# Attention by head pairs in plain single precision and row tiles, in a kernel of convolutions, attention and experts

## The chip, the cores and the metric

The kernel runs on one core of a Trainium2 chip. The time is that of the device in microseconds, from one execution of the program; lower is better. Engines are named as the profile names them: PE is TensorE, DVE is VectorE, ACT is ScalarE, POOL is GpSimd, SP is SyncE; PSUM is the memory that PE writes, in 8 banks of 512 single-precision columns.

## What is computed

The input is a batch of 8 images of 64 channels and 16 x 16 points (`B, C, HH, WW = 8, 64, 16, 16`). In order:

- group norm and a deformable 3 x 3 convolution (offsets and masks from a convolution of their own, four-corner interpolation), added to the input;
- group norm, a 3 x 3 convolution and a small mixing matrix that is balanced by 20 rounds of dividing its rows and columns by their sums (40 half steps); the result is a sum of the convolution, its input and the residual, weighted by the gates and by the trace of the balanced matrix;
- layer norm and causal attention with 8 heads over the 256 points of each image, added to the tokens;
- layer norm and a mixture of 8 experts (two are chosen a token, GELU), a windowed attention sum, layer norm, a mixture of 16 gated experts (SiLU), each added.

Attention, which the change is about, comes down to this for each image and head, where Y is the normed tokens (256 x 64) and A and M are products of weights (64 x 64) that the kernel makes itself once:

```python
q      = Y @ A[head]                      # query and key weights in one matrix
scores = (q @ Y.T) * 64 ** -0.5           # causal mask
probs  = softmax(scores)
out   += probs @ (Y @ M[head])            # value and output weights in one matrix
```

## The kernel before, in words

Every engine has its own list of instructions, written by hand in `hybrid_kernel`, and semaphores between them; nothing is reordered by a scheduler. What the lists have in common is a table of *fills*: pieces of work outside the step loop (projections, transposes, gate products) that `attention_fills(s)` assigns to a step, and that each engine's loop calls up at that step. All fills in `FILLS` share PSUM bank 7: a fill may be written when the one before it has been copied out (`take`, L1974: a wait for `misc_free`). Query and value projections with an odd index are *side* fills in bank 2, with semaphores of their own.

The stages that matter here:

**Tap loop** (PE L1893, 36 steps of 9 taps for 4 image pairs). DVE makes interpolation weights, PE transposes them into PSUM, ACT copies them (L908), PE multiplies (`interpolate`, L1861). DVE adds the result to each image pair (`x1_image`, L1217), and begins to balance the first mixing matrix (`half_steps(0, ...)`, L1282) in pieces whose borders are `HALVES`.

**Between tap loop and attention.** PE runs the first 3 x 3 convolution (`conv(0, ...)`, L1926: 9 taps, two passes each, bank 1), the products of the attention weights (`attention_weights`, L1939), which it runs twice so that ACT can split the result in a high part `AVH` and a low part `AVL`, and the second convolution (`conv(1, ...)`, bank 2). DVE balances to the end (L1359, L1361), adds the convolution (`add_conv`, L1363) and the residual (`second_residual`, L1376), takes the transposed tokens (`take_tokens`, L1381), norms them (`ln_center`, `ln_variance`, `ln_out`) and copies the transposed norm `yA` to `YTs` (`ln_evac`, L1440). Ten half steps of the second matrix are done on DVE as well; the other 30 belong to POOL and DVE together in the first 17 steps of attention: POOL adds up the sums, DVE takes the reciprocal (`inverse`, L1302), POOL multiplies (L637 to L655).

**Attention**, 64 steps s, one head of one image each (image a = s // 8, head g = s % 8). The order on PE (L2096) in step s: transposes of the probabilities of head s-1 (L2103, 3 tiles), scores of head s+1 (`scores`, L2082), probabilities times values of head s-2 (L2118 to L2120), then the fills of step s. Scores go to bank s % 2, transposes to banks 3 and 4, values to banks 5 and 6. DVE (L1568) masks and scales the scores and takes the row maximum (L1573, L1577: `masked_ready`), then does the fills of step s-1, norms, and the gates of tokens. ACT (L958) takes two exponentials with row sums (L968), copies the transposed probabilities of head s-1 to one of three buffers `PTs` (L953), then the projections of step s.

The norms, queries and attention weights are in a high and a low part that together fill the 128 rows (64 channels each): tokens `YTs` hold both, and a score tile is two accumulating matmuls with `QH` and `QL`. ACT copies a query projection to `QH` (L945), and DVE subtracts that from PSUM for `QL` (`query_remainders`, L1460, L1468). `normalise` (L1472) divides by the row sums, four heads at a time; POOL adds the heads up (`fold`, L711) and splits the expert weights (`split_stage`, L738).

**Experts** (PE L2197 on), behind the last mask. `gate_wide`, the buffer of spread gates that SP fills by DMA, lies over `QH`.

## Time and profile before

| | us |
|---|---|
| median of 3 runs | 490.46 |
| lowest and highest | 490.11, 490.84 |
| the profiled execution | 486.73 |
| its span, first to last instruction | 484.9 |

| chain of work that ended last | share of the span |
|---|---|
| PE | 63% |
| DVE | 16% |
| ACT | 8% |
| issue | 6% |
| POOL, DMA | 4%, 2% |

The granted PE clock is 0.98 of full speed on average, DMA moves 43 GB/s on average. The chain is followed back from the last instruction, at each step to what released it. Busy time is the time in which an engine has an instruction in work; matmuls are pipelined, and one that is recorded with 0.4 us may be followed by the next after 0.1. In a timeline row, the first number is the start in us from the span's start, the second how long the row lasts, then engine, line, operation, the tiles out<-in, sizes, and the count of instructions that were merged in the row; in brackets the idle time before it and who ended it. In a row by stage, each engine's busy time is followed by its number of instructions.

### The profile page before, as it was taken

To read this page: it belongs to the slowest core of one execution; us is meant where nothing else is said; L and a number is where in the kernel's file an instruction comes from. 1 tells how busy PE (TensorE), PEld (TensorE's weight loads), DVE (VectorE), ACT (ScalarE), POOL (GpSimd) and SP (SyncE) were. 2 spreads that over 40 slices of the span, in tenths; PEclk is the share of its full clock that TensorE was granted. 3 is DMA by queue.
4 is the path that set the end of the run, shared out by engine and by line. 5 is a ranking of instruction groups with operands and counts; after the bars stand their busy time and mean duration, and the time that the engine had idled before them with its cause. 6 is when DMAs were issued, how large, how long until landed. Compare 5 with 4: busy or idle time off the path is not lost.

```text
span 484.9 us, 9115 instructions
## 1 busy us (share of the span) xinstructions
PE 434.6 (90%) x2998; PEld 303.3 (63%) x2998; DVE 347.4 (72%) x1090; ACT 283.1 (58%) x676; POOL 175.6 (36%) x305
## 2 busy tenths in 40 slices
PE   2999999999968988979999988999989888998994
PEld 1787777767467887979898944344435444545542
DVE  4178998867777656788978853637666888797862
ACT  3467776732557876758788855765655333343431
POOL 4400001203134563383793342415341454343342
PEclk9998999999989998989999999999999999999998
DMA  7300000000400000012300004212112213041330
GB/s 178 144 2 1 2 0 1 1 2 0 87 3 1 1 2 1 2 39 51 69 20 3 1 3 141 63 39 68 43 38 74 68 45 105 28 122 66 99 102 11
DMA packets 13567, 20.94 MB, mean 43 GB/s; under 512 B 4592, under 2 KB 6384, under 8 KB 13008
## 3 DMA queue, kind: packets, MB, share of 16 engines
q1 hardware_dynamic: 13056, 19.99, 14.4%
q10 hardware_dynamic: 464, 0.37, 0.3%
q8 instruction: 24, 0.39, 0.3%
q14 instruction: 23, 0.19, 0.1%
HBM read 19.62 MB, written 0.72 MB: 42 GB/s over the span
## 4 chain that ended last, share of the span: by engine, by line
PE 63%; DVE 16%; ACT 8%; issue 6%; POOL 4%; DMA 2%; POOLq 0%; DVEq 0%; SPq 0%; ACTq 0%
PE PS L2171 14%; PE PS L1871 7%; PE PS L1909 6%; PE PS L2182 5%; PE PS L2193 5%; PE PS L1930 3%; PE PS L2103 3%; PE PS L2091 2%; PE PS L1829 2%; PE PS L1998 2%; PE PS L2013 2%; PE PS L2047 2%; ACT score_arena L968 2%; DVE QL L1468 2%; DVE score_arena L1577 2%
## 5 line engine op out<-in xcount | busy, mean ns | idle before, releaser
L2171 PE MATMUL PS<-YTs,WH 64*128 64x512 f32 x192 | 77.0, 427 | 1.9 <-ACT VV L1067 1.6
L735 POOL TENSOR_TENSOR pr<-pr 128x512 f32<-128x512 f32 x39 | 50.4, 1291 | 75.9 <-DVE pr L1630 44.7
L2171 PE MATMUL PS<-YX,WH 64*128 64x512 f32 x192 | 77.2, 426 | 0.0
L968 ACT ACTIVATE score_arena<-score_arena,nmx 128x128 f32<-128x128 f32 (+1 forms) x128 | 56.9, 446 | 22.2 <-DVE nmx L1577 21.8
L1067 ACT ACTIVATE VV<-PS 128x512 f32<-128x512 f32 x64 | 35.4, 595 | 41.6 <-PE PS L2171 41.5
L1023 ACT ACTIVATE stage<-PS,wk 128x512 f32<-128x512 f32 x64 | 40.8, 684 | 22.8 <-PE PS L2171 22.7
L1743 DVE TENSOR_TENSOR stage<-VV,PS 128x512 f32<-128x512 f32 x64 | 41.8, 682 | 17.1 <-ACT VV L1067 12.5
L2171 PEld LDWEIGHTS PS<-YTs,WH 64*128 64x128 f32 x192 | 35.3, 184 | 29.6 <-ACT VV L1067 12.6
L908 ACT ACTIVATE st_mem<-PS 128x512 f32<-128x512 f32 x72 | 37.3, 612 | 18.5 <-PE PS L1909 18.5
L2103 PE MATMUL PS<-cst,score_arena 128*128 128x128 f32 x192 | 34.4, 290 | 6.6 <-ACT score_arena L968 6.1
L2091 PE MATMUL PS<-YTs,QH 128*128 128x128 f32 (+1 forms) x128 | 38.9, 328 | 0.0
L2171 PEld LDWEIGHTS PS<-YX,WH 64*128 64x128 f32 x192 | 35.3, 184 | 4.0
L2171 PE MATMUL PS<-YX,WL 64*128 64x512 f32 x96 | 37.5, 391 | 0.0
L2171 PE MATMUL PS<-YTs,WL 64*128 64x512 f32 x96 | 37.5, 391 | 0.0
L2193 PE MATMUL PS<-stage,wk 128*64 128x512 f32 x128 | 34.5, 617 | 2.7 <-DVE stage L1743 2.7
L2091 PE MATMUL PS<-YTs,QL 128*128 128x128 f32 (+1 forms) x128 | 36.4, 285 | 0.0
L2182 PE MATMUL PS<-stage,wk 128*64 128x512 f32 x128 | 34.5, 617 | 1.6 <-ACT stage L1023 1.2
L1871 PE MATMUL PS<-st_mem,U 128*64 128x256 f32 x288 | 33.5, 383 | 0.0
L1323 DVE TENSOR_TENSOR prod<-hats 128x768 f32<-128x768 f32 x36 | 32.0, 949 | 0.1
L716 POOL TENSOR_TENSOR pr<-pr 128x512 f32<-128x512 f32 (+2 forms) x24 | 20.1, 837 | 32.9 <-DVE pr L1481 31.4
L953 ACT ACTIVATE score_arena<-PS 128x384 f32<-128x384 f32 x64 | 30.1, 471 | 0.9 <-PE PS L2103 0.9
L1468 DVE TENSOR_TENSOR QL<-PS,QH 128x512 fp32r<-128x512 f32 x32 | 22.0, 686 | 12.1 <-ACT QH L945 12.0
(277 smaller groups left out, 1130.1 us busy)
## 6 DMA issues: line engine op xcount, KB each, us to landing
QH<-gate_store SPq DMA_DIRECT2D x96, 128.0 KB, 2.9
stage<-in_wexp SPq DMA_DIRECT2D x6, 512.0 KB, 5.9
wk<-in_w SPq DMA_DIRECT2D x1, 1034.0 KB, 9.8
wa<-in_wat SPq DMA_DIRECT2D x1, 768.0 KB, 8.1
out<-X SPq DMA_DIRECT2D x16, 32.0 KB, 1.9
cst<-in_consts SPq DMA_DIRECT2D x1, 483.0 KB, 6.4
wc<-in_w SPq DMA_DIRECT2D x2, 183.5 KB, 5.8
score_arena<-in_wcv SPq DMA_DIRECT2D x2, 144.0 KB, 6.2
```

What stands on the lines that cost most here:

```text
L735: nc.gpsimd.tensor_tensor(acc[:, c % 2], acc[:, c % 2], weighted[:, u % 2], ALU.add).then_inc(acc_added, 1)
L908: nc.scalar.activation(ST[:, i % ST_TAPS, h].rearrange("p t s -> p (t s)"), PS[:, T_BANKS[m % 6], :], ACT.Copy).then_inc(st_copied, 1)
L968: ins = nc.scalar.activation(PR[:, s % 3, cols], MS[:, s % 3, cols], ACT.Exp, bias=nmx[:, s % 3, qt:qt + 1], scale=-1.0, accum_out=rsum[:, ...
L1023: nc.scalar.activation(hid[:, n % 4], PS[:, HID_BANKS[n % 4], :], ACT.Gelu, bias=wk[:, W128["b1"]][:, r:r + 1]).then_inc(gelu_done, 1)
L1067: nc.scalar.activation(sil[:, n % 4], PS[:, SILU_BANKS[n % 2], :], ACT.Silu).then_inc(silu_done, 1)
L1743: nc.vector.tensor_tensor(hid[:, n % 4], sil[:, n % 4], PS[:, V_BANKS[n % 3], :], ALU.mult).then_inc(prod3_done, 1)
L1871: ins = mm(PS[h * C:(h + 1) * C, 5 + j % 2, 0:S], U[:, 4 * j + 2 * qt + h, k * C:(k + 1) * C], ST[:, v % ST_TAPS, h, qt], start=(k + qt == ...
L2091: ins = mm(PS[:, s % 2, cols], w[:, a % 2, g, qt * P:(qt + 1) * P], YTs[:, a * S:a * S + (qt + 1) * P], start=(r == 0), stop=(r == 1))
L2103: ins = nc.tensor.transpose(PS[:, 3 + v % 2, k * P:(k + 1) * P], PR[:, v % 3, k * P:(k + 1) * P], ident)
L2171: ins = mm(PS[:, banks[i], :], w[hs, m, tiles[i] * P:(tiles[i] + 1) * P], ys[i][hs, cs], start=(k == 0), stop=(k == 2))
L2182: ins = mm(PS[i * C:(i + 1) * C, OUT_BANKS[u % 2], :], wk[:, W128["w2_2"]][:, r * C:(r + 1) * C], hid[:, (2 * q + i) % 4], start=(ht == 0) ...
L2193: ins = mm(PS[i * C:(i + 1) * C, OUT_BANKS[u % 2], :], wk[:, W128["w3"]][:, e * C:(e + 1) * C], hid[:, (2 * r + i) % 4], start=True, stop= ...
```

## The change

- Attention goes in 32 pairs of heads. Scores of a pair are plain single precision in two row tiles: head 2m in rows 0 to 63 and bank 0, head 2m+1 in rows 64 to 127 and bank 1. `Q`, `AV` and the tokens `YA` are single precision, `YA` with the same 64 channels in both halves. `QH`, `QL`, `AVH`, `AVL`, the second run of the attention weights and the query remainders are gone.
- An image has three projections (two of queries, one of values) instead of six, each two row-tiled matmuls in banks 6 and 7. There is no side bank: every fill takes the one slot.
- ACT takes all copies of fills in attention (projections, transposed norms and tokens, the second images' gates `gS` and trace `cB`), behind the exponentials of the next pair; DVE keeps the gate products `gB`, four steps late (`LAG`).
- Order on PE in pair m: scores of pair m+1, transposes of pair m, values of pair m-1, fills. On ACT: copies of pair m-1, exponentials of pair m, fills of pair m-1. On DVE: two masks, then all other work of the two steps (`background`).
- `PTs` has four buffers; transposes go to banks 2 and 3, values to banks 4 and 5.
- The first convolution runs inside the tap loop (after taps 33, 34, 35, bank 5). The second is split by the first projections; ACT copies half of its result aside (`HC`).
- All 40 half steps of the second matrix are POOL's with DVE's reciprocals, two a step over 20 steps; the gates of the second images come at s = 2.
- The first norms of attention are one DVE product (`ln_both`) instead of three operations. `gate_wide` has a buffer of its own.

Lines that are only "..." stand for what is left out.

```diff
-    return [("q", a, i) for i in range(HPAIRS)] + [("v", a, i) for i in range(PT)]
-
-
-def on_side(name):
-
-    return name[2] % 2 == 1
-
-
-DIAG_AT, XT_AT, YA_AT = 18, (20, 27), (7, 25, 38)
-DVE_HALVES = 10
-POOL_HALVES = tuple(min(40, DVE_HALVES + 2 * s - (s > 3) - (s > 4)) for s in range(19))
-MID_INVERSE, END_INVERSE = [s for s in range(17) if s != 4], [s for s in range(15) if s != 3]
+    return [("q", a, 0), ("q", a, 1), ("v", a, 0)]
+
+
+DIAG_AT, XT_AT, YA_AT = 20, (23, 30), (6, 27, 38)
+DVE_HALVES = 0
+GATES_AT = 6
+GATE_INVERSE_AT = 3
+LAG = 4
+LN_AT = ((2, 26, 34), (3, 27, 35), (5, 28, 37))
+ADD_AT, RESIDUAL_AT = 12, 24
+POOL_HALVES = tuple(min(40, 2 * s) for s in range(21))
+MID_INVERSE, END_INVERSE = range(20), range(20)
...
-    return {0: (2, 3, 4, 5, 6, 7), 3: (2, 3, 4, 5, 6, 7)}.get(a, (0, 1, 2, 3, 4, 5))
+    return {0: (2, 4, 6), 3: (5, 6, 7)}.get(a, (1, 3, 5))
...
+    if s == GATES_AT:
+        out.append(("gS", 0))
     if s == DIAG_AT:
         out.append(("cB", 0))
-    if s < 2:
-        out.append(("q", 0, 2 + s))
+    if s == 0:
+        out.append(("q", 0, 1))
+    if a + 1 < IMAGES and i in projections_at(a):
+        out.append(projections(a + 1)[projections_at(a).index(i)])
...
-HALVES = (8, 20, 25, 30, 36)
+HALVES = (6, 34, 38)
 PE_GROUP, PE_SQUARE, PE_COEF = 23, 26, 29
+CONV_AT = (33, 34, 35)
+CONV_SPLIT = (4, 5, 6)
...
-                        pool.wait_ge(balanced, 2)
+                    if n == 0:
+                        pool.wait_ge(exp_ready, 2)
...
+                if s == 2:
+                    batch_gates(1)
...
+            project(FIRST_PROJECTIONS[0])
+            batch_exp(1)
+            project(FIRST_PROJECTIONS[1])
+            copy_tokens(1)
...
+            for m in range(STEPS // 2 + 1):
+                if m >= 1:
+                    copy_probs(2 * m - 2)
+                    copy_probs(2 * m - 1)
+                if m == 1:
+                    act.wait_ge(conv_ready, 2)
+                    nc.scalar.activation(HC[:].rearrange("p j s -> p (j s)"), PS[:, 5, :], ACT.Copy).then_inc(conv_saved, 1)
+                if m < STEPS // 2:
+                    exponentials(2 * m)
+                    exponentials(2 * m + 1)
+                for s in (2 * m - 2, 2 * m - 1) if m >= 1 else ():
                     for name in attention_fills(s):
                         if name[0] in ("q", "v"):
                             project(name)
...
-            half_steps(0, HALVES[2], HALVES[3])
-            copy_square(1)
-            half_steps(0, HALVES[3], HALVES[4])
-            copy_logits(1)
-            half_steps(0, HALVES[4], 2 * SINKHORN)
+            half_steps(0, HALVES[2], 2 * SINKHORN)
...
+            def ln_both(c):
+
+                ts = ln_ready(c)
+                nc.vector.tensor_tensor(Y2[:, ts, 0:2 * C].rearrange("p t (r c) -> p t r c", r=2), Y[:, ts].unsqueeze(2).to_broadcast([P, CHUNK, 2, C]),
+                                        lnst[:, 2, ts].unsqueeze(2).unsqueeze(3).to_broadcast([P, CHUNK, 2, C]), ALU.mult).then_inc(y2_ready, 1)
...
             second_residual(0)
-            half_steps(1, 0, 2)
-            gate_inverse(1)
             take_tokens(0)
             ln_center(0)
             ln_variance(0)
-            ln_out(0, False)
+            copy_square(1)
+            ln_both(0)
             second_residual(1)
-            half_steps(1, 2, 4)
             ln_evac("yA", 0)
-            add_conv(2)
-            add_conv(3)
-
-            queries = [0]
-
-            def query_remainders(name):
-                _, a, i = name
-                queries[0] += 1
-                if on_side(name):
-                    dve.wait_ge(side_filled, SIDE[name] + 1)
-                else:
-                    dve.wait_ge(misc_filled, FILL[name] + 1)
-                dve.wait_ge(qh_copied, queries[0])
-                nc.vector.tensor_tensor(QL[:, a % 2, 2 * i:2 * i + 2, :].rearrange("p g n -> p (g n)"), PS[:, 2 if on_side(name) else 7, :],
-                                        QH[:, a % 2, 2 * i:2 * i + 2, :].rearrange("p g n -> p (g n)").bitcast(F32),
-                                        ALU.subtract).then_inc(side_free if on_side(name) else misc_free, 1)
+            copy_logits(1)
...
+            def background(s):
+
+                a, g = divmod(s, HEADS)
+                if s == GATE_INVERSE_AT:
+                    gate_inverse(1)
                 if s in MID_INVERSE:
                     inverse()
-                nc.vector.tensor_tensor_reduce(MS[:, s % 3, P:3 * P], PS[:, s % 2, P:3 * P], c_("causal"), -SCALE, 1e30,
-                                               ALU.add, ALU.min, nmx[:, s % 3, 1:2]).then_inc(masked_ready, 1)
-                if s >= 1:
-                    take_fills(s - 1)
-                if s == DIAG_AT + 1:
+                if s >= LAG:
+                    take_fills(s - LAG)
+                if s == ADD_AT:
+                    add_conv(2)
+                    add_conv(3)
+                if s == RESIDUAL_AT:
+                    dve.wait_ge(misc_free, FILL["cB", 0] + 1)
                     second_residual(2)
                     second_residual(3)
...
+            for m in range(STEPS // 2):
+                mask_scores(2 * m)
+                mask_scores(2 * m + 1)
+                background(2 * m)
+                background(2 * m + 1)
...
+                if i in CONV_AT:
+                    if i == CONV_AT[0]:
+                        pe.wait_ge(conv_block_loaded, 32)
+                        pe.wait_ge(x1_tile_ready, 3)
+                    n = CONV_AT.index(i)
+                    conv(0, n * TAPS // len(CONV_AT), (n + 1) * TAPS // len(CONV_AT))
...
             def project(name):
                 kind, a, i = name
-                if not on_side(name):
-                    take(*name)
-                elif SIDE[name]:
-                    pe.wait_ge(side_free, SIDE[name])
-                else:
-                    pe.wait_ge(conv_added, J)
-                bank = 2 if on_side(name) else 7
-                if kind == "q":
-                    for g in (2 * i, 2 * i + 1):
-                        for r, w in enumerate((AVH, AVL)):
-                            ins = mm(PS[:, bank, (g % 2) * S:(g % 2 + 1) * S], w[:, g * P:(g + 1) * P], YTs[:, a * S:(a + 1) * S],
-                                     start=(r == 0), stop=(r == 1))
-                else:
-                    for r, w in enumerate((AVH, AVL)):
-                        ins = mm(PS[:, bank, :], YTs[:, (2 * a + i) * P:(2 * a + i + 1) * P], w[:, 2 * 512:3 * 512], start=(r == 0), stop=(r == 1))
-                ins.then_inc(side_filled if on_side(name) else misc_filled, 1)
+                take(*name)
+                for r in range(2):
+                    rs = slice(r * C, (r + 1) * C)
+                    if kind == "q":
+                        g = 4 * i + 2 * r
+                        ins = mm(PS[:, 6 + r, 0:S], AV[rs, g * C:(g + 2) * C], YA[rs, a * S:(a + 1) * S], start=True, stop=True)
+                    else:
+                        ins = mm(PS[:, 6 + r, :], YA[rs, (2 * a + r) * P:(2 * a + r + 1) * P], AV[rs, 512:1024], start=True, stop=True)
+                ins.then_inc(misc_filled, 1)
...
             def scores(s):
                 a, g = divmod(s, HEADS)
-                if g % 2 == 0:
-                    wait_projection(("q", a, g // 2))
+                if g % 4 == 0:
+                    pe.wait_ge(misc_free, FILL["q", a, g // 4] + 1)
                 if s >= 2:
-                    pe.wait_ge(masked_ready, s - 1)
+                    pe.wait_ge(masked_ready, s)
                 for qt in range(PT):
                     cols = slice(0, P) if qt == 0 else slice(P, 3 * P)
-                    for r, w in enumerate((QH, QL)):
-                        ins = mm(PS[:, s % 2, cols], w[:, a % 2, g, qt * P:(qt + 1) * P], YTs[:, a * S:a * S + (qt + 1) * P],
-                                 start=(r == 0), stop=(r == 1))
-                ins.then_inc(scores_ready, 1)
-
+                    for h in range(2):
+                        hs = slice(h * C, (h + 1) * C)
+                        ins = mm(PS[:, h, cols], Q[hs, a % 2, g // 2, qt * P:(qt + 1) * P], YA[hs, a * S:a * S + (qt + 1) * P], start=True, stop=True)
+                        if qt == 1:
+                            ins.then_inc(scores_ready, 1)
+
+            transpose_x(0)
+            square_means(1)
+            conv(1, 0, CONV_SPLIT[0])
+            coefficients(1)
+            transpose_y("yA", 0)
+            conv(1, CONV_SPLIT[0], CONV_SPLIT[1])
+            pe.wait_ge(av_copied, 1)
+            pe.wait_ge(misc_free, FILL["yA", 0] + 1)
+            project(FIRST_PROJECTIONS[0])
+            conv(1, CONV_SPLIT[1], CONV_SPLIT[2])
             scores(0)
-            for s in range(STEPS + 2):
-                if 1 <= s <= STEPS:
-                    v = s - 1
-                    pe.wait_ge(probs_ready, v + 1)
-                    if v >= 2:
-                        pe.wait_ge(pT_copied, v - 1)
-                    for k in range(3):
-                        ins = nc.tensor.transpose(PS[:, 3 + v % 2, k * P:(k + 1) * P], PR[:, v % 3, k * P:(k + 1) * P], ident)
-                    ins.then_inc(pT_ready, 1)
-                if s + 1 < STEPS:
-                    scores(s + 1)
-                if s >= 2:
-                    v = s - 2
-                    a, g = divmod(v, HEADS)
-                    if g % 4 == 0 and a >= 1:
-                        pe.wait_ge(heads_normed, 2 * a - 1 + g // 4)
-                    if g == 0:
-                        wait_projection(("v", a, 0))
-                        wait_projection(("v", a, 1))
-                    pe.wait_ge(pT_copied, v + 1)
-                    vh = slice(g * C, (g + 1) * C)
-                    o = PS[:, 5 + g // 4, (g % 4) * P:(g % 4 + 1) * P]
-                    mm(o[:, 0:C], PTs[:, v % 3, 0:P], VV[:, a % 2, 0, vh], start=True, stop=True)
-                    mm(o[:, C:P], PTs[:, v % 3, P:2 * P], VV[:, a % 2, 0, vh], start=True, stop=False)
-                    mm(o[:, C:P], PTs[:, v % 3, 2 * P:3 * P], VV[:, a % 2, 1, vh], start=False, stop=True).then_inc(pv_done, 1)
-                if s < STEPS:
-                    for what in attention_fills(s):
-                        if what[0] in ("q", "v"):
-                            project(what)
-                        elif what[0] in ("yA", "yB", "zB"):
-                            transpose_y(*what)
-                        elif what[0] == "xT":
-                            transpose_x(what[1])
-                        elif what[0] == "cB":
-                            pe.wait_ge(v3_diag_ready, 2)
-                            take(*what)
-                            mm(PS[:, 7, 0:2], spread, V3[0:B, 1, BATCHES[1], 0], start=True, stop=True).then_inc(misc_filled, 1)
-                        else:
-                            pe.wait_ge(swl_ready, 3)
-                            small_projection(*what, "wg2", E2)
+            project(FIRST_PROJECTIONS[1])
+            conv(1, CONV_SPLIT[2], TAPS)
+            transpose_x(1)
...
+            for m in range(STEPS // 2 + 1):
+                if m + 1 < STEPS // 2:
+                    scores(2 * m + 2)
+                if m < STEPS // 2:
+                    transpose_probs(2 * m)
+                    transpose_probs(2 * m + 1)
+                if m >= 1:
+                    values(2 * m - 2)
+                    values(2 * m - 1)
+                if m < STEPS // 2:
+                    for s in (2 * m, 2 * m + 1):
+                        for what in attention_fills(s):
+                            fill_attention(what)
```

## Rows read from the trace of the kernel before

**Rows 1.** The page: busy us, share of the span and instructions of each engine.

```profile
PE 434.6 (90%) x2998; PEld 303.3 (63%) x2998; DVE 347.4 (72%) x1090; ACT 283.1 (58%) x676; POOL 175.6 (36%) x305
```

**Rows 2.** Busy time by stage: length, each engine, then clock and DMA.

```profile
138.20:184.90 46.70, 41.66 (x323) 38.67 (x323) 30.79 (x143) 35.91 (x117) 23.74 (x100) 0.96 0.01 2
184.90:262.70 77.80, 70.77 (x560) 66.73 (x560) 62.66 (x247) 58.90 (x197) 47.70 (x75) 0.96 0.13 29
262.70:276.50 13.80, 13.35 (x118) 12.78 (x118) 12.20 (x60) 12.07 (x46) 5.14 (x6) 1.00 0.01 2
```

**Rows 3.** PE timeline, one step without fills (start us, us, what).

```profile
265.17 0.50 PE L2103 MATMUL PS<-cst,score_arena 128*128 128x128 f32 x3
265.42 0.30 PE L2091 MATMUL PS<-YTs,QH 128*128 128x128 f32 x1
...
265.97 0.33 PE L2118 MATMUL PS<-VV,score_arena 128*128 128x64 f32 x2
...
266.58 0.50 PE L2103 MATMUL PS<-cst,score_arena 128*128 128x128 f32 x3
```

**Rows 4.** DVE timeline ahead of attention: balancing done, tokens, residual, first mask.

```profile
120.23 0.22 DVE L1361 TENSOR_SCALAR V<-cst,V 8x4 f32<-8x4 f32 x1
...
123.45 0.36 DVE L1384 COPY T<-PS 128x256 f32<-128x256 f32 x1
...
127.45 0.48 DVE L1378 SCALAR_TENSOR_TENSOR X<-score_arena,CB,X 128x256 f32<-128x256 f32 x1
...
138.15 0.29 DVE L1573 CUSTOM_DVE_ANT_0 score_arena<-PS,cst 128x128 f32<-128x128 f32 x1
```

**Rows 5.** ACT timeline: the first exponential.

```profile
139.05 0.40 ACT L968 ACTIVATE score_arena<-score_arena,nmx 128x128 f32<-128x128 f32 x1 [3.38 <-DVE nmx L1577]
```

**Rows 6.** Chain that ended last: first convolution passes, first expert products.

```profile
106.41 3.63 PE PS L1930 x8
...
279.82 0.91 PE PS L2171 x6
```

**Rows 7.** PE timeline of the weights' product: lower and upper row group.

```profile
111.30 0.27 PE L1944 MATMUL PS<-wa 64*128 64x128 f32 x1
111.35 0.27 PE L1949 MATMUL PS<-wa 64*128 64x64 f32 x1
111.41 0.27 PE L1944 MATMUL PS<-wa 64*128 64x128 f32 x1
```

**Rows 8.** PE timeline of the expert stage: row-tiled pairs after another shape.

```profile
304.11 0.50 PE L2171 MATMUL PS<-YTs,WH 64*128 64x512 f32 x1
...
304.44 0.39 PE L2171 MATMUL PS<-YTs,WL 64*128 64x512 f32 x1
...
304.68 0.39 PE L2171 MATMUL PS<-YX,WH 64*128 64x512 f32 x1
```

**Rows 9.** DVE timeline in attention: a mask's start, the remainder behind it.

```profile
147.87 0.29 DVE L1573 CUSTOM_DVE_ANT_0 score_arena<-PS,cst 128x128 f32<-128x128 f32 x1
...
148.43 0.69 DVE L1468 TENSOR_TENSOR QL<-PS,QH 128x512 fp32r<-128x512 f32 x1
```

**Rows 10.** ACT timeline in attention: exponentials, probabilities, query copy.

```profile
148.55 0.40 ACT L968 ACTIVATE score_arena<-score_arena,nmx 128x128 f32<-128x128 f32 x1 [0.34 <-DVE nmx L1577]
...
149.44 0.47 ACT L953 ACTIVATE score_arena<-PS 128x384 f32<-128x384 f32 x1
149.81 0.58 ACT L945 ACTIVATE QH<-PS 128x512 fp32r<-128x512 f32 x1
```

**Rows 11.** DVE timeline: multiplications of two half steps that follow each other.

```profile
134.55 0.16 DVE L1293 TENSOR_TENSOR ef<-ef,mn 8x16 f32<-8x16 f32 x1
...
135.15 0.18 DVE L1293 TENSOR_TENSOR ef<-ef,mn 8x16 f32<-8x16 f32 x1
```

**Rows 12.** POOL timeline: multiplications of two half steps, with DVE.

```profile
149.82 0.21 POOL L654 TENSOR_TENSOR ef<-ef,mn 8x16 f32<-8x16 f32 x1 [0.28 <-DVE mn L1306]
...
150.84 0.21 POOL L654 TENSOR_TENSOR ef<-ef,mn 8x16 f32<-8x16 f32 x1 [0.28 <-DVE mn L1306]
```

339 lines of the change are left out of this document (167 added, 172 removed).

## The prediction, made before the changed kernel was run

> Notation: PE is TensorE, DVE VectorE, ACT ScalarE, POOL GpSimd, SP SyncE. A step is one head of one image (64 of them, s = 0 to 63), a pair is two steps (m = 0 to 31). A fill is a projection, transposition or gate product that PE slips between the steps.
>
> **What bounds the kernel now.** First the page's busy times: PE works 434.6 us of a span of 484.9, 90% [rows 1], so the question is where its time goes and where it still waits. Then busy time by stage, with the borders at the first mask of step 0, that of step 20, and the exponentials of steps 54 and 63 [rows 2]: in steps 0 to 19 PE works 41.7 of 46.7 us, in steps 20 to 53 70.8 of 77.8, and neither DVE (62.7) nor ACT (58.9) is full. So attention is bound by hand-overs between three engines that are each rather full. Then the PE timeline of one step without fills [rows 3]: transposes at 265.17, scores at 265.42, values at 265.97, next step at 266.58: 0.25 + 0.55 + 0.61 = 1.41 us. The last 9 steps, which have almost no fills, take 13.8 / 9 = 1.53 us [rows 2], 8% over that. With fills a step takes about 77.8 / 34 = 2.3 us. Ahead of attention, DVE carries the end: the first balancing is done at 120.23, tokens are taken at 123.45, the layer norm is out by 127.45, and the first mask comes at 138.15 [rows 4], the first exponential at 139.05 [rows 5]. Attention ends where the expert stage's first product starts, at 279.82 [rows 6]. Behind that I expect nothing to change: the same code, the same banks but for the fills' second one, the gate copies in a buffer of their own but still behind the same wait for the scores. So the sum goes to that point and the shift is carried to the end.
>
> **The change, part by part.**
>
> Scores. Before, two accumulating 128-row passes a tile, 0.55 us a head [rows 3]. After, plain single precision with 64 rows a head, so each product is two passes (the tile's high and low weights). Passes of this kind are in the trace, in the weights' product: upper and lower row group each start one every 0.11 us, and both do at once (111.30, 111.35, 111.41) [rows 7]. A pass over 512 columns takes 3.63 / 8 = 0.45 [rows 6], so one over 256 is 0.21 to 0.23. A pair's scores are then 2 x 0.11 + 2 x 0.22 = 0.65 us with both heads side by side, against 1.10. Changing from whole rows to row tiles is not free: in the expert stage the first row-tiled pair after another shape lasts 0.33 to the next, later ones 0.24 (304.11, 304.44, 304.68) [rows 8]. I charge 0.1 on entering and 0.1 on leaving: 0.85 a pair.
>
> The Trainium skill has a rule against this change: TensorEngine Tiling (Array Packing), Key Properties, says that changing the tiling mode, as against the tile, drains TensorE. The trace agrees that something is paid, 0.1 us each way [rows 8]; what a full drain would make of the time stands with the rivals.
>
> PE per pair without fills: transposes 0.50 + values 1.22 + scores 0.85 = 2.57, against 2.82. Fills: a query projection is now 2 passes of 256 columns in both row groups, 0.43 + 0.2 = 0.63, two an image; values 2 of 512, 0.86 + 0.2 = 1.06, one an image. Before it was 4 and 2 with twice the passes.
>
> DVE loses the query remainders, 30 x 0.69 = 20.7 us in attention (the code has 32, two of them ahead of it), and the copies of transposed tokens and norms. It keeps the masks: from 147.87 to 148.43, 0.56 a step [rows 9]. ACT gets those copies, about ten of 0.58 or less, and loses half of the query copies. Its pair: exponentials 2 x 0.89, probabilities 2 x 0.37 (148.55, 149.44, 149.81) [rows 10] = 2.5, and with fills 3.3. PE with fills is at 2.57 + 15.4 / 22 = 3.3 (below). So PE and ACT are level, and DVE drops out, except in the first 20 steps.
>
> Start. The first convolution (9 taps, 18 passes, 8.2 us [rows 6]) goes ahead of the end of the tap loop, where PE is full: the loop ends 8.2 us later, and DVE balances beside it instead of after (28 half steps before the last image instead of 12 by the code). The second pass of the attention weights goes, and a third of the columns of the first. I get the first balancing done at about 119.4 (0.8 earlier). To the tokens two half steps and a gate reciprocal fall out: 121.8 instead of 123.45. The norm is out 0.6 sooner, as one product replaces three operations: 125.3, the residual 125.7. Transposing 0.5, copying 0.65, a convolution tap 0.9 and a projection 0.63, its copy 0.58, a tap and the scores: first mask at about 129.4, against 138.15 [rows 4]. The six half steps that DVE did just ahead of the mask (135.15 - 134.55 = 0.6 each, 3.6) are now POOL's [rows 11], and the wait for remainders is gone. But behind the scores PE has the value projection and three taps (1.06 + 2.7), then the second image's tokens, and ACT copies these before its first exponential: 134.1. Against 139.05 [rows 5] that is **-5.0 us**.
>
> First 20 steps. All 40 half steps of the second balancing now run between POOL and DVE; one takes 150.84 - 149.82 = 1.02 us [rows 12], of which DVE does one reciprocal. DVE's queue in a pair is mask, mask, then the reciprocals of two steps, four in all, each waiting for POOL; behind them are the next masks, for which ACT and then PE wait. A pair therefore lasts at least 1.12 + 0.1 + 3 x 1.02 = 4.3 us, whatever PE does (3.3). That is no better than 2 x 2.1 before. POOL's gates at s = 2 and the norm's power at s = 3 stand in the same queue and hold DVE some 2.2 us more; pair 3 has three fills on one bank, each of which PE may only write when ACT has emptied the one before: 1.6 more. Carried through by hand: pair 1's scores wait behind the three taps, its masks end at 135.4, three more half steps and the 2.2 make the mask of step 4 start at about 141; then 8 pairs of 4.3 and 2.6 of other waits, step 20 at about 178, against 184.9 [rows 2]: -6.9 in all, so **-1.9 us** here.
>
> Steps 20 to 63. PE: 22 x 2.57 = 56.5. Fills: 8 query (5.0), 5 value projections (5.3), 7 norm transposes and 3 gate products at some four passes of 0.11 (4.5), small ones 0.6: 15.4. Fills in the same pair wait for ACT, whose order is copies, both exponentials, then fills: the second fill is held until 0.5 + 1.78 + 0.58 = 2.9 us after the transposes, where PE would be at 1.8; 1.1 lost, later ones 0.4 to 1.0 each. Pair 10 has two fills (1.2), pair 15 five (3.1), pair 16 two and waits for a gate that DVE empties four steps late (2.0), pairs 23 and 24 alike (1.1 + 2.0), and in pairs 13 and 14 two norms fall together on DVE (2.2): 11.6. With the last copies and values (2.0) and 1.1 from step 20's mask to PE's next scores: 178 + 1.1 + 56.5 + 15.4 + 11.6 + 2.0 = 264.6. The 8% that the last 9 steps showed over the bare PE work would add up to 5.8; pairs have some 1.2 us between ACT's readiness and PE's arrival, which steps had not, so I take half: 267.5, against 279.82: **-12.3 us** in all, 5.4 of it here. Bounds: -15.2 with none of the 8%, -21 if half of the hand-over stalls are hidden as well; -3 if DVE's first stage also delays by one whole half step a pair (10 us).
>
> Costed at nothing: the copy of the convolution's result (ACT, 0.6, while it waits for masks; if that cover is gone, 0.6); SP's expert loads start some 5 us earlier, under DMA that is idle here; the wider values copy replaces two.
>
> Sum: the profiled execution took 486.73 us, span 484.9; -12.3 gives 474.4. The median shown, 490.46, lies 3.7 above the profiled one; 490.46 - 12.3 = **478.2 us**.
>
> **The rivals.**
>
> Stalls hidden (0.17): PE finds its fills' bank free. For it: with DVE relieved, masks and exponentials come early. Against: ACT's order puts fills last. Gain 12.3 + 2.9 + 5.8 = 21: 469.
>
> Slower: the row groups do not overlap for pairs of two-pass products of two shapes (0.08). Place: scores and projections. A pair's scores would be 1.33 + 0.2, +0.68; an image's fills +1.7. The first stage, DVE-bound, absorbs it; 22 x 0.68 + 5 x 1.7 = 23.5: 478.2 + 23.5 = 502. It decides from half of the overlap on: at 12 us lost the gain is gone. Against: [rows 7], where the second group starts while the first still has passes to run.
>
> Slower: a drain at each change of shape (0.06). If each change waits out the whole of the last product, 0.39 from its record instead of the 0.24 after which the next may start [rows 8], it costs 0.15 more, and nearer 0.26 with the first pair's 0.1; four changes a pair, 22 pairs: 0.15 to 0.26 x 88 = 13 to 23: 491 to 501. The rule of the Trainium skill (TensorEngine Tiling (Array Packing), Key Properties), taken at its word, would give this.
>
> No change (0.06): DVE's queue in the first stage loses one half step a pair (10 us) and the fills' stalls are a fifth larger: 490. For it: everything DVE does behind a late reciprocal is late too. Against: POOL goes on while DVE masks.
>
> The forecast has 0.63. All that is below 489.5 counts as faster: 0.63 + 0.17 = **0.80**; same 0.06; slower 0.14. A measurement of this kernel tells apart about 0.2%, 1 us. The range, 466 to 492, takes in the bounds and the near rivals; 502 and a gain over 24 us are left out.
>
> **What would show it.** Right: scores of a pair about 0.65 us with both row groups starting together; pairs of 4.2 to 4.4 us to step 20, with DVE waiting for POOL; from there 3.3 to 3.7, under 2.8 at the end; PE waiting ahead of second fills; first exponential near 134; the stretch behind attention still 205 us. Wrong: score passes one after the other; step 20's mask later than 185; PE waiting for exponentials in most pairs after step 20, which would mean that DVE or ACT, not PE, sets the pair.

## The result, and the profile after

The changed kernel takes 509.8 us (median of four; 502.3 to 512.5) against 490.3 for the kernel before: a ratio of 1.035, interval 1.029 to 1.042. **Slower, by 19.5 us in the medians, where 478.2 us was predicted.** The profiled execution took 509.7 us, its span is 507.6 us and its mean granted clock 0.922. Ratios, here and below, leave out executions that were disturbed, so one can differ from that of two medians.

The page's busy times (the line of [rows 1]) show less work on DVE and ACT, and 12.4 us more of it on PE than before:

```profile
PE 447.0 (88%) x2898; PEld 288.6 (57%) x2898; DVE 318.7 (63%) x1018; ACT 276.5 (54%) x661; POOL 182.9 (36%) x335
```

The windows of the changed kernel (columns as in [rows 2]), with borders at the first mask, at that of step 20, and at the first product of the experts, with the 27 us from 203.0 apart; then the last two stretches in the kernel before:

```profile
130.80:183.60 52.80, 45.00 (x302) 33.26 (x300) 23.00 (x135) 35.21 (x116) 26.52 (x125) 0.87 0.01 2
...
203.00:230.30 27.30, 22.69 (x95) 16.43 (x96) 7.23 (x33) 10.50 (x31) 12.09 (x20) 0.50 0.16 39
...
183.60:297.50 113.90, 98.58 (x680) 77.90 (x678) 63.38 (x284) 72.43 (x244) 58.31 (x92) 0.83 0.08 20
297.50:507.60 210.10, 188.29 (x1097) 93.50 (x1096) 138.47 (x337) 96.98 (x170) 77.95 (x71) 0.95 0.21 64
```

```profile
184.90:279.80 94.90, 87.42 (x704) 82.57 (x703) 76.47 (x311) 72.83 (x247) 52.83 (x81) 0.96 0.11 24
279.80:484.90 205.10, 181.74 (x1097) 90.53 (x1096) 138.39 (x337) 97.16 (x170) 77.98 (x71) 0.99 0.21 66
```

The column to read is the last but two, the clock. From step 20 to the experts it is 0.83, in one stretch of 27.3 us it is 0.50: the lower of the engine's two levels, 1.2 in place of 2.4 GHz. A mean of 0.83 over 113.9 us means that 2 x 0.17 x 113.9 = 39 us ran at the lower one. Before, the same stretch took 94.9 us at 0.96.

The marks that the prediction named, from the ACT, DVE and PE timelines (first exponential, mask of step 20, first expert product), beside [rows 5, 2, 6]:

```profile
134.98 0.39 ACT L977 ACTIVATE score_arena<-score_arena,nmx 128x128 f32<-128x128 f32 x1
```

```profile
183.64 0.29 DVE L1577 CUSTOM_DVE_ANT_0 score_arena<-PS,cst 128x128 f32<-128x128 f32 x1 [0.31 <-issue]
```

```profile
297.45 0.79 PE L2184 MATMUL PS<-YTs,WH 64*128 64x512 f32 x1
```

And PE's timeline around that stretch. The bracket is the wait ahead of the instruction and what ended it:

```profile
203.66 1.11 PE L2003 MATMUL PS<-cst,Y 128*128 128x128 f32 x4 [2.76 <-DVE Y L1456]
204.70 1.65 PE L2071 MATMUL PS<-YA,Q 64*128 64x128 f32 x8
206.28 1.54 PE L2096 MATMUL PS<-cst,score_arena 128*128 128x128 f32 x6
```

PE waits 2.76 us for the third chunk's norm. Behind the wait, eight score passes take 1.65 us and the six transposes 1.54, where the same groups take 0.93 and 0.87 at the full clock (below). So the first suspicion: the waits that the change makes cost more than their own length.

### The profile page after: what moved, and what is told of

It reads as the page before. It is cut to its first block, busy times and chain, and to the rows that moved or that the text cites. A ratio compares the mean times of both kernels' runs of the same rounds, so it can differ in the third digit from the quotient of the medians.

```text
span 507.6 us, 8805 instructions
## 1 busy us (share of the span) xinstructions
PE 447.0 (88%) x2898; PEld 288.6 (57%) x2898; DVE 318.7 (63%) x1018; ACT 276.5 (54%) x661; POOL 182.9 (36%) x335
## 4 chain that ended last, share of the span: by engine, by line
PE 63%; DVE 13%; ACT 10%; POOL 7%; issue 5%; DMA 1%; POOLq 0%; DVEq 0%; ACTq 0%; SPq 0%
PE PS L2184 14%; PE PS L1894 6%; PE PS L1944 6%; PE PS L2195 5%; PE PS L2206 5%; PE PS L2071 4%; PE PS L1924 4%; ACT score_arena L977 3%; PE PS L2003 3%; PE PS L2096 2%; PE PS L1852 2%; PE PS L2015 2%; DVE score_arena L1579 2%; PE PS L2175 2%; PE PS L2045 1%
## 5 line engine op out<-in xcount | busy, mean ns | idle before, releaser
L2184 PE MATMUL PS<-YTs,WH 64*128 64x512 f32 x192 | 80.0, 442 | 1.9 <-ACT VV L1090 1.6
L2184 PE MATMUL PS<-YX,WH 64*128 64x512 f32 x192 | 80.0, 442 | 0.0
L2184 PEld LDWEIGHTS PS<-YTs,WH 64*128 64x128 f32 x192 | 36.7, 191 | 30.8 <-ACT VV L1090 12.6
L1046 ACT ACTIVATE stage<-PS,wk 128x512 f32<-128x512 f32 x64 | 40.8, 684 | 22.9 <-PE PS L2184 22.7
L1577 DVE CUSTOM_DVE_ANT_0 score_arena<-PS,cst 128x128 f32<-128x128 f32 x64 | 18.5, 289 | 49.2 <-PE PS L2071 48.8
L959 ACT ACTIVATE score_arena<-PS 128x384 f32<-128x384 f32 x64 | 28.8, 485 | 22.7 <-PE PS L2096 22.0
L2071 PE MATMUL PS<-YA,Q 64*128 64x128 f32 (+1 forms) x256 | 33.3, 386 | 8.7 <-DVE nmx L1579 5.4
L2184 PEld LDWEIGHTS PS<-YX,WH 64*128 64x128 f32 x192 | 36.7, 191 | 4.2
L2206 PE MATMUL PS<-stage,wk 128*64 128x512 f32 x128 | 35.5, 633 | 2.7 <-DVE stage L1766 2.7
L2195 PE MATMUL PS<-stage,wk 128*64 128x512 f32 x128 | 35.5, 633 | 0.1
L2096 PEld LDWEIGHTS PS<-cst,score_arena 128*128 128x128 f32 x192 | 23.6, 157 | 15.1 <-issue 9.8
L2071 PEld LDWEIGHTS PS<-YA,Q 64*128 64x128 f32 x256 | 20.9, 217 | 18.0 <-issue 6.4
```

Source lines behind the costliest of these rows:

```text
L1046: nc.scalar.activation(hid[:, n % 4], PS[:, HID_BANKS[n % 4], :], ACT.Gelu, bias=wk[:, W128["b1"]][:, r:r + 1]).then_inc(gelu_done, 1)
L2071: ins = mm(PS[:, h, cols], Q[hs, a % 2, g // 2, qt * P:(qt + 1) * P], YA[hs, a * S:a * S + (qt + 1) * P], start=True, stop=True)
L2096: ins = nc.tensor.transpose(PS[:, 2 + v % 2, k * P:(k + 1) * P], PR[:, v % 3, k * P:(k + 1) * P], ident)
L2184: ins = mm(PS[:, banks[i], :], w[hs, m, tiles[i] * P:(tiles[i] + 1) * P], ys[i][hs, cs], start=(k == 0), stop=(k == 2))
L2195: ins = mm(PS[i * C:(i + 1) * C, OUT_BANKS[u % 2], :], wk[:, W128["w2_2"]][:, r * C:(r + 1) * C], hid[:, (2 * q + i) % 4], start=(ht == 0) ...
L2206: ins = mm(PS[i * C:(i + 1) * C, OUT_BANKS[u % 2], :], wk[:, W128["w3"]][:, e * C:(e + 1) * C], hid[:, (2 * r + i) % 4], start=True, stop= ...
```

## Experiments

Theory A: the loss is TensorE's clock, which falls behind waits. Theory B: it is the waits. Theory C: single precision in row tiles is slow by itself. "Throw-away matmuls" below are products of 128 x 128 into columns of PSUM that nothing reads, as the kernel has them already in its first stage.

**1. The clock held up, no wait removed.**

```diff
...
+def awake(at, v):
+    for _ in range(AWAKE.get(at, 0)):
+        mm(PS[:, 4 + max(v, 0) % HEADS // 4, 384:512], ident, cst[:, 0:P], start=True, stop=True)
...
+                    awake(2 * m + 2, 2 * m - 4)
                     scores(2 * m + 2)
...
+                            awake(what, 2 * m - 2)
                             fill_attention(what)
```

`AWAKE` says how many products go ahead of which scores or fill; its 14 places stand in the edit of experiment 2.

> The changed kernel with throw-away 128x128 matmuls added on TensorE just ahead of fourteen of its longest waits in attention (10 ahead of the scores that wait for the second query projection, 11 ahead of the third chunk's transposes, 9 ahead of the scores of step 46, 2 to 5 ahead of the others), some 65 of them at 0.20 us each at full rate. No wait is removed. Theory A (the granted clock falls after TensorE's waits, and the half-rate stretches are most of the loss): the half-rate stretches of attention shrink from 62 us to under 20, the mean granted clock rises from 0.92 to 0.97 or more, the experts start at 275 to 285 in place of 297.5, and the time falls to 482 to 495. Theory B (the waits themselves are the loss, the clock only goes with it): the clock may rise, but the time stays at 500 to 515, as the waits end when they did or later. Theory C (plain single precision in row tiles is slow by itself): as B.

490.2 us, 0.996 of before (0.993 to 1.000), clock 0.979: **19.6 us came back by adding work.** PE's timeline at one of the places (20 passes are ten products), and the windows with the borders used above; the last row is the throw-away matmuls alone from step 20 on:

```profile
138.33 0.70 PE L2013 MATMUL PS<-YA,AV 64*128 64x256 f32 x4
138.96 2.50 PE L2079 MATMUL PS<-cst 128*128 128x128 f32 x20
141.69 0.93 PE L2071 MATMUL PS<-YA,Q 64*128 64x128 f32 x8 [0.23 <-ACT Q L940]
```

```profile
131.80:182.20 50.40, 46.33 (x342) 35.32 (x342) 22.94 (x135) 35.14 (x116) 26.52 (x125) 0.97 0.01 2
182.20:281.70 99.50, 93.57 (x768) 76.81 (x766) 63.35 (x284) 71.97 (x244) 58.32 (x92) 1.00 0.10 22
281.70:488.00 206.30, 183.44 (x1097) 91.16 (x1096) 138.37 (x337) 97.14 (x170) 77.98 (x71) 0.98 0.21 66
```

```profile
182.20:281.70 99.50, 12.20 (x90) 10.82 (x90) 1.00 0.10 22
```

In the changed kernel the scores at this place came at 140.72, behind a wait of 2.65 us; here the products stand in the wait, 0.23 us of it is left, and the scores still start when the projection is copied. Nothing else differs, and from step 20 to the experts the clock is 1.00 and 14.4 us are gone. Theory A's numbers hold (experts at 281.7, time inside 482 to 495), B's and C's do not. But the experts still start 14 us later than predicted, so A is not all.

**2. One place alone**, ahead of the third chunk's transposes (the wait of 2.76 us).

```diff
-AWAKE = {4: 10, ('v', 1, 0): 4, ('yA', 1): 4, 18: 3, 22: 3, ('yA', 2): 11, ('xT', 3): 3, ('yB', 0): 2,
-         ('v', 4, 0): 3, ('gB', 0): 4, ('yA', 3): 3, 46: 9, ('gB', 1): 4, ('gB', 2): 3}
+AWAKE = {('yA', 2): 11}
```

> The changed kernel with throw-away matmuls at one place alone: 11 ahead of the third chunk's transposes, before which TensorE waits 2.76 us and behind which its clock stays at half rate for 27 us. Theory A: that stretch goes or shrinks to under 10 us, the 16 to 27 us given back at full rate are worth 8 to 13 us, the other falls stay: 496 to 502. If a stretch of such length comes from the small waits inside it (0.5 to 1.2 us each), it stays at 15 us or more, and the time at 503 to 511.

499.9 us (496.5 to 505.1), in the medians 9.9 less than the changed kernel; by the ratios to the kernel before, 1.021 and 1.035, it is 7. The PE timeline at the place, and the 27.3 us that had run at 0.50:

```profile
199.43 2.67 PE L2079 MATMUL PS<-cst 128*128 128x128 f32 x22
202.36 0.66 PE L2003 MATMUL PS<-cst,Y 128*128 128x128 f32 x4 [0.25 <-DVE Y L1456]
```

```profile
203.00:230.30 27.30, 22.09 (x125) 16.06 (x124) 9.92 (x47) 13.19 (x39) 12.52 (x22) 0.71 0.18 39
```

A's time, but only in part A's picture: the fall at 203 is gone, and another comes at 214.6, among the five fills of pair 15, where waits of 1.0, 0.6 and 0.7 us stand ahead of it. A mean of 0.71 leaves 2 x 0.29 x 27.3 = 16 us at the lower level, which is the expectation's other case (15 us or more). Filling one wait gives back some 7 to 10 us and leaves a fall among shorter ones.

**3. ScalarE's order.** The fills of pair m-1 taken before the exponentials of pair m.

```diff
-                if m < STEPS // 2:
-                    exponentials(2 * m)
-                    exponentials(2 * m + 1)
                 for s in (2 * m - 2, 2 * m - 1) if m >= 1 else ():
...
+                if m < STEPS // 2:
+                    exponentials(2 * m)
+                    exponentials(2 * m + 1)
```

> The changed kernel with one thing moved: ScalarE takes the fills of pair m-1 before, and not after, the exponentials of pair m. Nothing is added or removed. Theory B (TensorE waits because ScalarE takes the fills last): the waits ahead of the second fill of a step and of the scores that need a projection shorten by the 2.2 us of four exponentials, the experts start 8 to 15 us earlier, the time is 492 to 502. Theory A: shorter waits leave the clock up as well, so the time falls by more, to 480 to 495. Rival: the exponentials now wait for a fill that TensorE issues last in its step, the transposes of each pair come later, and the time rises to 515 or more.

535.7 us, 1.088 of before (1.080 to 1.096): the rival. PE's waits of attention by line (us in total, times, longest), and the stretch from step 20 on:

```profile
PE PS L2096 <- ACT score_arena L977: 21.7, 37, 1.3
```

```profile
195.00:328.60 133.60, 108.04 (x696) 84.11 (x696) 63.74 (x284) 75.86 (x252) 56.62 (x87) 0.82 0.08 17
```

PE now waits for exponentials 37 times, 21.7 us in all, and the clock is 0.82. With one fill buffer, "fills last" is the better order.

**4. Four buffers undone** in kernel 1, that of experiment 1 (the same index in the value products).

```diff
-    if v >= 4:
-        act.wait_ge(pv_done, v - 3)
-    nc.scalar.activation(PTs[:, v % 4, :], PS[:, 2 + v % 2, 0:384], ACT.Copy).then_inc(pT_copied, 1)
+    if v >= 3:
+        act.wait_ge(pv_done, v - 2)
+    nc.scalar.activation(PTs[:, v % 3, :], PS[:, 2 + v % 2, 0:384], ACT.Copy).then_inc(pT_copied, 1)
```

> The first experiment's kernel (clock held up by throw-away matmuls, 490.2 us) with one part of the change undone: three buffers of transposed probabilities in place of four. ScalarE's second copy of a pair then waits for the first value product of the pair before, which TensorE issues just behind the transposes. If the fourth buffer does little: 490 to 494 (up to 0.1 us a pair). If it is what lets a pair's stages follow without a wait: 0.3 us or more in each of 32 pairs, 500 us or more.

504.7 us against kernel 1's 490.2: the expectation's second case (500 or more). A pair without fills, kernel 1 and then this one (PE timeline):

```profile
266.22 0.93 PE L2071 MATMUL PS<-YA,Q 64*128 64x128 f32 x8
267.08 0.87 PE L2102 MATMUL PS<-cst,score_arena 128*128 128x128 f32 x6
267.79 0.33 PE L2117 MATMUL PS<-VV,score_arena 128*128 128x64 f32 x2
...
269.17 0.38 PE L2071 MATMUL PS<-YA,Q 64*128 64x128 f32 x2
```

```profile
276.48 0.93 PE L2071 MATMUL PS<-YA,Q 64*128 64x128 f32 x8
277.39 0.55 PE L2102 MATMUL PS<-cst,score_arena 128*128 128x128 f32 x3
278.26 0.55 PE L2102 MATMUL PS<-cst,score_arena 128*128 128x128 f32 x3 [0.33 <-ACT score_arena L977]
...
280.02 0.38 PE L2071 MATMUL PS<-YA,Q 64*128 64x128 f32 x2
```

2.95 us a pair become 3.54: ACT's copy waits for values, its exponentials come later, and PE waits 0.33 us between the two groups of transposes. The fourth buffer is worth 0.6 us in this pair, which the prediction had not priced, though not in each: the pair before takes 2.84 us in both kernels. From step 20 to the experts it is 111.9 us (182.0 to 293.9) for 99.5, with a clock of 0.94 for 1.00; of the 12.4 us, 0.06 x 111.9 = 6.7 at most can be the clock; the rest is waiting.

**5. Fills moved apart**, by constants (`MOVED` gives a fill a new step and overrides `attention_fills`).

```diff
+MOVED = {('gS', 0): 14, ('v', 1, 0): 8, ('q', 2, 0): 9, ('xT', 3): 25, ('v', 4, 0): 32}
-ADD_AT, RESIDUAL_AT = 12, 24
+ADD_AT, RESIDUAL_AT = 18, 24
```

> The changed kernel with fills moved apart: the gate spread from pair 3 to pair 7 (its addition on VectorE from step 12 to 18), the value projection of image 1 from pair 3 to 4, the token transposes of the last tile from pair 15 to 12, the value projection of image 4 from pair 15 to 16, so that pair 3 has one fill in place of three and pair 15 three in place of five. Theory B (coincident fills on one buffer): pairs 3 and 15 lose 8 to 12 us of waiting and half-rate work, the time is 496 to 503. Theory A: the falls of the clock after pairs 3 and 15 go (up to 34 us at half rate), the time is 485 to 497. If neither matters, 507 to 513.

Median 496.8 us, but single executions from 489.7 (clock 0.968) to 505.0 (0.925); the ratio is 1.003 (0.997 to 1.009). That is inside A's range and at the lower end of B's, so only the profile can tell them apart. In the profiled execution (492.2 us) the experts start at 282.3 and the clock from step 20 on is 0.97, without throw-away matmuls. That stretch, and the fill behind the third chunk's norm:

```profile
182.20:282.30 100.10, 85.47 (x676) 68.68 (x674) 63.48 (x284) 71.89 (x244) 58.19 (x91) 0.97 0.10 22
```

```profile
200.58 0.66 PE L2012 MATMUL PS<-cst,Y 128*128 128x128 f32 x4 [2.54 <-DVE Y L1465]
```

PE is still idle for 14.6 us of it (100.10 - 85.47), where the changed kernel has 15.3 (113.90 - 98.58), and the third chunk's wait is still 2.54 us. But here the scores behind that wait take 0.93 us (201.17), so no fall came with it, and 13.8 us are gone. So it is not the waiting in all, nor this wait by itself, that sets the clock; what else does is not shown.

**6. One wait priced**, in kernel 1: DVE empties the gate logits two steps after their fill.

```diff
-LAG = 4
+LAG = 2
```

> The first experiment's kernel (clock held up by throw-away matmuls) with one constant changed: VectorE takes the gate logits two steps after their fill, not four, so the one fill buffer comes free a pair earlier. With the clock out of the way this prices one wait. Theory B's part (the buffer held by the logits makes TensorE wait in pair 16, whose period was 9.82 us there): that period falls to 5 to 7 us, the experts start at 277 to 279.5 in place of 281.7, the time is 486 to 488.5 against the first experiment's 490.2. If the period is set by something else it stays at 9 or more, and the time at 489 to 491.

489.5 us, no change, and from one pair's scores at 206.63 to the next at 216.46 it still takes 9.83 us: the logits did not hold it. The PE timeline between shows what does, five fills on one buffer and up to 1.3 us between each and the next (throw-away matmuls, L2079, in the waits):

```profile
209.58 0.70 PE L2013 MATMUL PS<-YA,AV 64*128 64x256 f32 x4
...
211.31 0.41 PE L1992 MATMUL PS<-cst,X 128*128 128x128 f32 x2 [0.16 <-ACT Q L940]
...
213.60 1.13 PE L2015 MATMUL PS<-AV,YA 64*128 64x512 f32 x4
214.66 1.16 PE L2079 MATMUL PS<-cst 128*128 128x128 f32 x8
215.94 0.58 PE L2024 MATMUL PS<-sw,YTs 128*128 128x16 f32 x4
```

**7. The fills laid out anew.** No throw-away matmuls; one fill a pair nearly everywhere.

```diff
+MOVED = {('q', 1, 0): 1, ('q', 1, 1): 2, ('v', 1, 0): 4, ('yA', 1): 6, ('q', 2, 0): 9, ('q', 2, 1): 11, ('v', 2, 0): 13,
+         ('gS', 0): 14, ('q', 3, 0): 17, ('q', 3, 1): 19, ('cB', 0): 20, ('xT', 2): 23, ('v', 3, 0): 24, ('xT', 3): 25,
+         ('yA', 2): 27, ('q', 4, 0): 29, ('q', 4, 1): 31, ('v', 4, 0): 32, ('yB', 0): 33, ('q', 5, 0): 35, ('gB', 0): 36,
+         ('q', 5, 1): 38, ('v', 5, 0): 40, ('yA', 3): 41, ('q', 6, 0): 43, ('q', 6, 1): 44, ('yB', 1): 47, ('v', 6, 0): 48,
+         ('q', 7, 0): 50, ('gB', 1): 52, ('q', 7, 1): 54, ('v', 7, 0): 56, ('zB', 0): 58, ('zB', 1): 60}
-ADD_AT, RESIDUAL_AT = 12, 24
+ADD_AT, RESIDUAL_AT = 18, 22
-LAG = 4
+LAG = 2
-SPLIT_AT = (25, 33, 41)
+SPLIT_AT = (25, 33, 43)
-LN_AT = ((2, 26, 34), (3, 27, 35), (5, 28, 37))
+LN_AT = ((2, 24, 34), (3, 25, 35), (5, 26, 37))
-FIRST_PROJECTIONS = [("q", 0, 0), ("v", 0, 0)]
+FIRST_PROJECTIONS = [("q", 0, 0), ("v", 0, 0), ("q", 0, 1)]
...
```

> The changed kernel with no throw-away matmuls and with its fills laid out anew: one fill a pair nearly everywhere, each query projection filled two pairs ahead of the scores that read it, the gate logits taken after two steps, the second query projection of image 0 ahead of the first pair, the routing's middle pieces four steps later and the third split of the weights two. Theory B (the waits were coincident or late fills): no wait of TensorE over 2 us is left but that for the third chunk, steps 20 to 63 take 88 to 95 us as the prediction had it, the experts start at 268 to 276. Theory A: with the waits gone the clock holds by itself at 0.965 or more, and the time is 475 to 485. If waits only move to other places, 487 to 500.

486.2 us, 0.995 of before (0.992 to 0.999): a little faster than before, though over A's 485, with a clock of 0.964 where A had 0.965 or more. B's stage times hold; its waits do not, as one over 2 us is left that is not the third chunk's. Its windows from step 20 on, and its longest wait of attention:

```profile
180.60:273.80 93.20, 83.60 (x681) 68.45 (x680) 63.18 (x284) 71.59 (x244) 58.48 (x91) 0.97 0.11 24
273.80:484.10 210.30, 188.60 (x1097) 93.29 (x1096) 138.39 (x337) 96.97 (x170) 77.92 (x71) 0.95 0.21 64
```

```profile
PE PS L2000 <- ACT VV L949: 2.9, 1, 2.9
```

The steps of the routing (37, 38 and 42, and 16 later) move to 41, 42 and 46. The experts start at 273.8, 6 us earlier than before; but their stretch takes 210.3 us where it took 205.1, at a clock of 0.95 against 0.99. The wait of 2.9 us that is left is a second fill in one pair (pair 12). The same with throw-away matmuls ahead of six waits:

```diff
+AWAKE = {18: 3, 22: 3, ('yA', 2): 6, ('q', 4, 1): 3, 46: 4, 50: 3}
```

> The kernel with the fills laid out anew, and throw-away matmuls ahead of six waits that it may keep (6 ahead of the third chunk's transposes, 3 or 4 ahead of the scores of steps 18, 22, 46 and 50 and of one query projection). Theory A: as the layout alone, with fewer falls of the clock left, so 0 to 5 us faster than it and less spread between runs: 473 to 482. If the layout alone leaves no fall, equal to it within 1.5 us or slower by up to 2 (the added matmuls take 4.4 us in all, part of it outside a wait).

487.5 us, 1.3 above the layout alone and, by the two intervals, not told apart from it; A's 473 to 482 is missed. The wait of pair 12 was not among the six.

**8. Does the clock also lengthen the experts?** The layout with the clock held, in two tries: the first line of each pair below is the first try's, the second the second's (`LATE` is the same thing for the experts' fills, in the fills' own bank and behind the wait for it).

```diff
+for _ in range(9):
+    mm(PS[:, 6, 384:512], ident, cst[:, 0:P], start=True, stop=True)
 pe.wait_ge(v3_diag_ready, 1)
...
+AWAKE = {('yA', 2): 13, ('gB', 2): 3, ('q', 4, 1): 3}
+AWAKE = {('gB', 2): 3}
...
+LATE = {("yC", 0): 9, ("yC", 2): 4, ("yD", 2): 4, ("wC", 3): 3}
+LATE = {("yD", 1): 9, ("yC", 2): 4}
```

> The kernel with the fills laid out anew (486.2 us, four falls of the clock in the expert stretch, one at the start of attention, one at its end), and throw-away matmuls ahead of the waits that those falls follow: 9 ahead of the diagonal's spread at 117 us, 13 ahead of the third chunk's transposes, 3 ahead of the last gate logits, and 9, 4, 4 and 3 ahead of four fills of the expert stretch. Theory A: most of the half-rate stretches go (35 us in that profile, some 25 of them at these places), the expert stretch falls from 210.3 back to 206 or less, the clock is 0.98 or more, the time 477 to 483. If the expert stretch is longer for another reason than the clock, it stays at 209 to 211 us and the time at 484 to 488.

489.4 us: a miss. The largest groups stood ahead of fills that waited for nothing, so they added some 4 us, and the experts took 210.8 us. Put where the trace shows the waits (9 products ahead of the diagonal's spread, 3 ahead of the last gate logits, 9 and 4 ahead of the two transposes of the experts that wait 2.1 and 0.9 us):

> The kernel with the fills laid out anew (486.2 us, clock 0.964, expert stretch 210.3 us against 205.2 in the kernel of before), and throw-away matmuls at four places where its trace shows a wait just ahead of a fall: 9 ahead of the diagonal's spread at 117 us, 3 ahead of the last gate logits at 270 us, 9 and 4 ahead of the two transposes of the expert stretch that wait 2.1 and 0.9 us (the try before had its largest groups ahead of other fills, where they filled no wait and added 4 to 5 us). Theory A: the expert stretch is longer only by its falls, so it comes down to 205 to 208 us, the clock is 0.975 or more, the time 479 to 484. If the stretch is longer for another reason, it stays at 209 to 211 and the time at 484.5 to 488.

484.1 us, 0.985 of before (0.983 to 0.988), **the fastest of the study**, at the upper end of A's range. The stretches from step 20 and of the experts:

```profile
180.80:274.70 93.90, 84.45 (x682) 69.53 (x680) 63.16 (x284) 71.73 (x244) 58.49 (x92) 0.96 0.11 24
274.70:481.90 207.20, 186.40 (x1123) 94.36 (x1122) 138.45 (x337) 97.14 (x170) 77.92 (x71) 0.98 0.20 65
```

In the profiled executions the experts' stretch came down by 3.1 us to 207.2, with its clock from 0.95 to 0.98, though products were added in it.

**9. The kernel before, with its clock held**, in two tries again.

```diff
 for what in attention_fills(s):
+    if what == ("yA", 2):
+        pe.wait_ge(side_free, SIDE["v", 3, 1] + 1)
+    for _ in range({("xT", 2): 8, ("yA", 2): 13}.get(what, 0)):
+        mm(PS[:, 5 if what[0] == "xT" else 2, 384:512], ident, cst[:, 0:P], start=True, stop=True)
...
+    for _ in range({("xT", 2): 8, ("yB", 0): 13}.get(what, 0)):
+        mm(PS[:, 5 if what[0] == "xT" else 6, 384:512], ident, cst[:, 0:P], start=True, stop=True)
```

The first try's 13 go to the side bank, with a wait for it; its trace shows no idle time of PE there. The second try's go to bank 6, without such a wait.

> The kernel of before with throw-away matmuls ahead of two of its own waits (8 ahead of the third tile's transposes, 13 ahead of the third chunk's), after each of which its granted clock falls for 3.4 us. Theory A (a wait costs its half-rate stretch besides itself, in the kernel of before too): the two stretches go, the clock rises to 0.985 or more, and the time falls by 1 to 4 us, to 486 to 489. If the clock follows something other than TensorE's waits, both stretches stay and the time is 489.5 to 492.

491.0 us (ratio 1.004, 1.000 to 1.008): a miss. Thirteen of the products stood ahead of a fill without a wait and took 3.1 us (195.68 to 198.8). With them ahead of the wait:

> The kernel of before with throw-away matmuls ahead of the two waits that its clock falls after: 8 ahead of the third tile's transposes, and 13 ahead of the first transposes of the experts' tokens (the earlier try had put these ahead of another fill, where TensorE did not wait). Theory A: neither fall is left in attention but the one at its start, the granted clock is 0.985 or more, and the time falls by 1 to 4 us against before, to 486 to 489. If the falls stay, 489 to 491.

487.7 us, inside A's range, but a ratio of 0.997 (0.994 to 1.001): not told apart from no change, and the clock of 0.979 is under A's 0.985. The windows, steps 20 on and the experts:

```profile
186.20:279.20 93.00, 88.95 (x745) 84.34 (x744) 76.25 (x311) 72.83 (x247) 52.92 (x81) 1.00 0.11 24
279.20:488.60 209.40, 186.37 (x1097) 91.91 (x1096) 138.80 (x337) 97.08 (x170) 77.95 (x71) 0.97 0.20 65
```

Attention gains 1.9 us (93.0 for 94.9, clock 1.00 for 0.96), and the experts lose 4.3 (209.4 for 205.1, clock 0.97 for 0.99) in the profiled execution, by falls that the kernel before had not shown in its own. The two profiled executions took 490.4 and 486.7 us, where the medians are 487.7 and 489.3.

## Why the prediction was wrong

By its own stages, in microseconds of the profiled execution (predicted span 484.9 - 12.3 = 472.6):

| | before | predicted | after | 1: clock held | 7: layout | layout, held |
|---|---|---|---|---|---|---|
| to the first exponential | 139.1 | 134.1 | 135.0 | 135.9 | 137.2 | 137.4 |
| to the mask of step 20 | 45.8 | 43.9 | 48.6 | 46.3 | 43.4 | 43.4 |
| to the experts | 94.9 | 89.5 | 113.9 | 99.5 | 93.2 | 93.9 |
| experts, to the end | 205.1 | 205.1 | 210.1 | 206.3 | 210.3 | 207.2 |
| span | 484.9 | 472.6 | 507.6 | 488.0 | 484.1 | 481.9 |

**Right: the start.** -4.1 us for -5.0. **Right: the row tiles.** The heads' score passes overlap: a pair's scores take 0.86 us (266.22 to 267.08 in kernel 1) where 0.85 was charged. That refutes the first of the two slower rivals. The second, a wait for the whole of the last product at each change of shape, is refuted too: in kernel 1's timeline, leaving the row tiles and entering them again, the next group starts before the last record ends (267.08 before 267.15, 269.17 before 269.25):

```profile
266.77 0.38 PE L2071 MATMUL PS<-YA,Q 64*128 64x256 f32 x2
267.08 0.33 PE L2102 MATMUL PS<-cst,score_arena 128*128 128x128 f32 x1
```

```profile
268.97 0.28 PE L2119 MATMUL PS<-VV,score_arena 128*128 128x64 f32 x1
269.17 0.38 PE L2071 MATMUL PS<-YA,Q 64*128 64x128 f32 x2
```

But 0.2 us a pair was too little. Leaving takes 0.31 where a pass of 256 columns takes 0.21, entering 0.20 where a pass of 64 takes 0.11, and the first pass behind each change is longer by 0.05 and 0.10: some 0.34 a pair. The rival's rule came from the Trainium skill (TensorEngine Tiling (Array Packing), Key Properties), by which a change of tiling mode drains TensorE; the trace bears out a price of 0.15 to 0.2 us a change.

None of the prediction's three signs of being wrong came: the row groups start together, step 20's mask comes at 183.6, and behind it PE waits for exponentials twice, 0.5 us in all.

**Wrong, and the step that failed: the waits of steps 20 to 63, "11.6", were charged at their own length, and all work at the full clock.** The stretch was 24.4 us longer than predicted (113.9 for 89.5). Kernel 1 splits this. Of its 99.5 us PE was busy 93.6, 12.2 of it with throw-away matmuls, so the change's own work there is 81.4 us at the full clock, and 18.1 us are not its work. The changed kernel has the same work, but is busy 98.6 us with it:

- half-rate work: 98.6 - 81.4 = **17.2 us**, charged at nothing;
- PE's work at the full clock: 81.4 where 56.5 + 15.4 = 71.9 was charged, **+9.5**. A pair without fills takes 2.95 (266.22 to 269.17), not 2.57: transposes 0.71 for 0.50, values 1.38 for 1.22. The 0.25 that was read from [rows 3] for three transposes is the time to the scores behind them, which start 0.03 us behind the last; among themselves these passes follow each other after 0.11, so six take 0.66 and the change of shape 0.05; of the values' 0.16, the change of shape is 0.09. Over 22 pairs that is up to 8.4; the rest is in the fills;
- waits: 113.9 - 98.6 = 15.3 where 89.5 - 71.9 = 17.6 was charged (11.6, 2.9 for hand-overs, 2.0 and 1.1 at the ends), **-2.3**.

Busy time runs to the recorded end of a product, some 0.2 us past the point where the next could start, so the border between work and waits is soft by that much a wait; the sum is not.

The waits themselves were sized well (the four between pair 15's five fills are 0.79, 0.56, 0.69 and 1.22 us in the changed kernel, 3.3 where 3.1 was charged). And 17.2 us fits the clock: 39 us at half rate can cost at most 19.5. What the waits did to the clock was not in the sum. The row that could have told stood in the prediction's own group: [rows 2] give a granted clock of 0.96, not 1.00, in both stretches of attention before, and 1.00 in the one stretch with hardly a wait (13.35 of 13.80 us busy). The kernel before lost clock behind waits too, the longest of them 3.0 us:

```profile
PE PS L1998 <- ACT VV L947: 3.0, 1, 3.0
```

```profile
208.88:211.85 2.97, 0.00 (x1) 0.03 (x1) 2.90 (x9) 1.84 (x6) 2.89 (x6) 0.99 0.00 0
211.85:215.20 3.35, 3.35 (x17) 3.35 (x17) 2.81 (x12) 1.48 (x5) 3.35 (x6) 0.50 0.00 0
```

The change made more waits (15.3 us from step 20 on, against 94.9 - 87.4 = 7.5 before); that it has one buffer for fills where there were two is argued from experiments 6 and 7, not shown by itself.

**Wrong: the first 20 steps**, 48.6 for 43.9. Kernel 1 has 46.3 with a clock of 0.97, so 2.3 of the 4.7 went with the clock. The rest is the fills of the first pairs: the layout, with the second query projection early and single fills in pairs 0 to 7, takes 43.4, and pairs 4 to 8 of it take 4.2 to 4.4 us each, as the bound of 4.3 had it.

**Wrong: "behind that I expect nothing to change".** Same code, same waits (PE's longest in the experts' stretch is 2.2 us before and after, and this one 2.1), yet 5.0 us more. One place, the wait and then what follows it, in the kernel before and in the changed one:

```profile
360.36:362.46 2.10, 0.00 (x0) 0.00 (x0) 1.28 (x1) 0.73 (x2) 1.77 (x2) 1.00 0.33 75
362.46:366.00 3.54, 3.54 (x23) 2.01 (x24) 0.93 (x2) 2.81 (x4) 0.99 (x1) 1.00 0.53 178
```

```profile
378.49:380.61 2.12, 0.00 (x1) 0.00 (x1) 1.29 (x1) 0.74 (x2) 1.78 (x2) 0.98 0.33 98
380.61:384.10 3.49, 3.49 (x12) 1.51 (x14) 0.42 (x1) 1.88 (x2) 0.00 (x0) 0.52 0.55 166
```

The same wait of 2.1 us is followed by 1.00 before and by 0.52 after. Filling such waits gave back 3.1 us in experiment 8. Part of the 5.0 can be the execution that was profiled: the kernel before took 486.7 us in it, while its medians beside the experiments are 489.3 to 490.2, most executions at a clock of 0.975 to 0.979. In the other profiles the same expert code takes 206.3 to 210.9 us. Why a wait brings the clock down in one kernel or execution and not in another stays open: nothing tried here moves a wait alone in time.

The whole: 507.6 - 472.6 = 35.0 us too short by the spans (31.6 by the medians). Of them 19.6 went when the clock was held and nothing else was touched (kernel 1). The other 15.4 stand in the table's column of kernel 1: 10.0 in steps 20 to 63, nearly all of it PE's undersized work, 2.4 in the first 20 steps, 1.8 ahead of them, 1.2 in the experts.

The rivals: "stalls hidden" and "no change" asked what the waits are worth at one clock, and the true case, waits that slow the work behind them, was none of the four. The Trainium skill has such a case: TensorE: Matmul & The Clock Gate, in "A second HAM failure mode: psum-queue depth-cycling", tells of a kernel in which TensorE idles briefly between groups of matmuls, so often that the clock goes back and forth between its levels, at a cost to throughput. The trace agrees in kind: 15.3 us of waits went with 17.2 us of slower work. On that page the median matmul kept its time at the full clock; here whole groups took 1.8 times theirs.

## What to carry to other kernels

Where TensorE bounds a stage, read the granted clock beside its waits: a wait can have a second price, the half-rate work behind it, which here was as large as the waits themselves, and a change that saves passes but adds short waits can lose by it. To find that price, put throw-away matmuls into the waits that the trace shows, and only there: in the wait they cost next to nothing (experiment 1), a fill earlier they cost their full length (3.1 us in experiment 9). Laying out the work anew, here one fill a pair on the single buffer and each query projection two pairs ahead of its reader, gave 486.2 us without them and 484.1 with the clock held as well. One profiled execution is not enough to compare clocks by: the falls differ between executions of one kernel.

## What the hardware showed that was not expected

- At the lower level both groups that were compared are slower alike, 1.8 times: scores 1.65 us for 0.93, transposes 1.54 for 0.87 (PE timelines above). A busy stretch of 27 us stayed at that level throughout, with PE busy 22.7 of 27.3 us.
- The clock fell behind short waits as well: in experiment 2 at 214.6, with waits of 0.9, 1.0, 0.6 and 0.7 us in the 8 us ahead of it and none longer in the 11 us ahead.
- The same wait can be followed by either level: the third chunk's, 2.76 us in the changed kernel and 2.54 in experiment 5, by 27.3 us at the lower level and by none.
- Executions of one kernel spread with the clock: those of experiment 5's kernel took 489.7 us at 0.968 to 505.0 at 0.925. Those of kernel 1 took 488.3 to 491.0.
